# A fused attention block on one Trainium2 core: eight low-part operations given to GpSimd, one small result put in another PSUM bank, and every table of slots rewritten

## The reference, cut to what matters

```python
xn = layernorm(x)                                  # per row
q  = (layernorm(xn) * norm_g + norm_b) @ Wq        # 16 heads of 64
k, v = split(xn @ Wkv)
k, v = concat(null_k, k), concat(null_v, v)        # 2 more columns
q, k = l2norm(q) * q_scale, l2norm(k) * k_scale
sim  = 8 * q @ k.T - slope[h] * distance           # causal
x + softmax(sim) @ v @ Wout + layernorm(...)*ln_g + ln_b
```

## Time and profile before

| | us |
|---|---|
| median of 3 runs | 2699.43 (2696.95 to 2702.16) |
| the profiled execution | 2701.09 |
| its span | 2699.3 |

### The profile page before, as it was taken

One profiled execution on the slowest core, in us unless ns is written; L12 is line 12 of the kernel. 1 busy time (PEld: TensorE's weight loads), 2 busy tenths in 40 slices (PEclk: granted clock), 3 DMA queues, 4 the chain that ended last, 5 costly groups with the idle time before them and its releaser, 6 DMA issues.

```text
span 2699.3 us, 84329 instructions
## 1 busy us (share of the span) xinstructions
PE 2627.6 (97%) x31631; PEld 1578.7 (58%) x31631; DVE 2483.1 (92%) x6756; ACT 2127.0 (79%) x3385; POOL 2103.5 (78%) x2442
## 2 busy tenths in 40 slices
PE   5899999999999999999999999999999999999997
PEld 4456556565565565565565565566555665565654
DVE  8999998999989999999999999999999999989996
ACT  5688887888877888877888878788887888877876
POOL 6677887779867788678877788778887778877774
PEclk7899999999999999999999999999999999999999
DMA  5333354334544344433443436443453434544222
GB/s 170 74 67 72 79 105 98 89 73 82 100 100 94 69 87 97 98 85 78 96 103 82 89 75 102 102 92 72 78 106 89 101 71 78 100 102 74 57 56 71
DMA packets 638789, 236.94 MB, mean 88 GB/s; under 512 B 594608, under 2 KB 596656, under 8 KB 638384
## 3 DMA queue, kind: packets, MB, share of 16 engines
q1 hardware_dynamic: 636912, 231.45, 40.4%
q10 hardware_dynamic: 1472, 0.09, 0.0%
HBM read 72.01 MB, written 16.78 MB: 33 GB/s over the span
## 4 chain that ended last, share of the span: by engine, by line
PE 84%; DVE 7%; DMA 3%; issue 3%; POOL 2%; SPq 1%; ACT 1%; ACTq 0%; POOLq 0%; DVEq 0%
PE PS L1268 13%; PE PS L1245 12%; PE PS L1246 11%; PE PS L1247 11%; PE PS L1292 6%; PE PS L1331 6%; PE PS L1335 4%; PE PS L1333 4%; PE PS L1272 4%; PE PS L1358 4%; PE PS L1359 4%; PE PS L1360 4%; DVE PS L1044 2%; PE PS L1303 1%; DVE QKB L1064 1%
## 5 line engine op out<-in xcount | busy, mean ns | idle before, releaser
L1044 DVE CUSTOM_DVE_ANT_0 PS<-PS,STR 128x512 f32<-128x512 f32 (+3 forms) x1536 | 822.5, 580 | 124.3 <-PE PS L1292 117.4
L598 ACT ACTIVATE AR<-PS,SC 128x1024 f32<-128x1024 f32 (+1 forms) x640 | 655.0, 1023 | 146.5 <-PE PS L1303 76.8
L1245 PE MATMUL PS<-WH,XT 128*128 128x388 f16 x2048 | 677.3, 331 | 20.7 <-DVE AR L1057 10.8
L1246 PE MATMUL PS<-WL,XT 128*128 128x388 f16 x2048 | 674.6, 329 | 0.0
L1247 PE MATMUL PS<-WH,XT 128*128 128x388 f16 x2048 | 674.2, 329 | 0.0
L602 ACT ACTIVATE AR<-AR 128x1024 f16<-128x1024 f32 (+1 forms) x640 | 621.7, 971 | 20.3
L810 POOL TENSOR_TENSOR RN<-SS,HALF 128x8 f32<-128x8 f32 x256 | 453.6, 1772 | 179.2 <-DVE SS L1132 178.0
L1085 DVE TENSOR_TENSOR AR<-AR 128x768 f16<-128x768 f32 (+1 forms) x448 | 503.1, 1134 | 13.2 <-ACT AR L602 13.2
L1268 PE MATMUL PS<-AR 64*128 64x512 f16 (+3 forms) x4608 | 496.7, 324 | 9.2 <-ACT AR L598 9.2
L1331 PE MATMUL PS<-AR 128*128 128x66 f16 x4608 | 473.0, 195 | 2.1 <-DVE AR L1085 1.2
L1333 PE MATMUL PS<-AR 128*128 128x64 f16 x4608 | 469.4, 192 | 0.0
(11 more groups left out here) (227 smaller groups left out, 5199.7 us busy)
## 6 DMA issues: line engine op xcount, KB each, us to landing
XW<-in_L_attn_x SPq DMA_DIRECT2D x112, 256.0 KB, 3.1
XB<-in_L_attn_x SPq DMA_DIRECT2D x64, 256.0 KB, 2.9
out<-ACC SPq DMA_DIRECT2D x64, 256.0 KB, 2.3
ACC<-in_L_attn_x SPq DMA_DIRECT2D x56, 256.0 KB, 3.0
AR<-QKB SPq DMA_TRANSPOSE x512, 2.5
AR<-in_L_attn_Wkv SPq DMA_DIRECT2D x2, 1536.0 KB, 12.7
ACC<-in_L_attn_x SPq DMA_DIRECT2D x2, 1024.0 KB, 7.1
AR<-in_L_attn_Wout SPq DMA_DIRECT2D x1, 2048.0 KB, 8.3
```

The source lines that it names most:

```text
L598: e.activation(PR[:, n % 2, :, 0:wide], SB[:, :, 0:wide], ACT.Exp, scale=SIG).then_inc(s_p, 1)
L1044: e.tensor_tensor_reduce(out=r[:, 0:n], in0=r[:, 0:n], in1=ST[:, u % 2, h, o:o + n], scale=1.0, scalar=LOW, op0=ALU.add, op1=ALU.max, accu ...
L1245: e.matmul(to, XT[:, k, xs], WH[:, k, p, :], start=k == 0, stop=False)
L1246: e.matmul(to, XT[:, k, xs], WL[:, k, p, :], start=False, stop=False)
```

## The change

Three things. First, the low parts 8 to 15 of the late weights (the q weights of pairs 2 to 7) go from VectorE, one operation each, to GpSimd, two operations each: a multiplication in place and a subtraction. Their counts go to a semaphore of their own, `s_spq`, on which unit 1's turns into `KQ` and unit 2's first projection now wait. Second, the small transpose and product of the weights' maxima go to bank 5, and the transpose no longer waits until ScalarE has emptied the bias columns from bank 2. Third, all tables are new, `HOLD` too; the numbers of entries stay, apart from `W_LATD` and `W_LATP`.

```diff
@@ -48,68 +48,69 @@
 STEPS = [(qc, [(kt, 0)]) if kt < 4 * qc + 2 else (qc, [(kt, 0), (kt + 1, 256)]) for qc in range(2) for kt in range(4 * qc + 3)]
 NS = len(STEPS)
 PL_POOL = (0, 4, 7)
-W_PIECE = [47, 53, 56, 59, 66, 68, 69, 77, 79, 82, 83, 86]
-W_MAX = [41, 45, 49, 55, 64, 64, 66, 72, 75, 75, 76, 84]
-W_SCORE = [88, 96, 105, 108, 111, 115, 118, 126, 130, 133]
-W_PLOW = [94, 100, 101, 105, 108, 115, 122, 125, 131, 135]
-W_VALUE = [108, 109, 110, 116, 124, 127, 130, 136, 141, 149]
-W_NVP = [105, 115]
...
-W_OP = [121, 121, 138, 149, 160, 160, 167, 170]
-W_ADD = [117, 118, 136, 142, 158, 159, 167, 167]
-W_PROJ = [z for z in [7, 10, 17, 22, 26, 31, 37, 43] for k in range(KC)]
-W_KV = [5, 10, 16, 22, 28, 33, 39, 41]
-W_VL = [3, 7, 16, 21, 24, 27, 40, 42]
...
-W_SS = [13, 23, 36, 47]
-W_POW = [15, 28, 44, 47]
-W_TP = [25, 28, 59, 66]
-W_HI = [30, 37, 54, 68]
-W_LO = [26, 34, 52, 67]
...
-W_STAT = [-288, -194, -181, -174, -128, -113, -101, -96]
-W_XB = [-84, -74, -48, -28, -5, 8, 15, 17]
-W_XF = [-73, -53, -29, -6, -6, 11, 18, 20]
-W_XH = [-64, -25, -25, -4, 14, 14, 25, 28]
-W_XL = [-65, -33, -18, -4, 0, 10, 24, 25]
...
-HOLD = [2.0, 2.1, 2.0, 6.7]
...
-W_LATA = [-364, -352, -337, -320, -233, -223, -210, -207, -204, -202, -194, -152, -136, -103, -66, -55]
-W_LATD = [-313, -246, -231, -193, -187, -179, -171, -128, -96, -89, -73, -68, -67, 17, 19, 20]
-W_XF0 = [-177, -170]
-W_XH0 = [-73, 2]
-W_XL0 = [-78, -1]
-W_XT0 = [-106, -11]
-W_WOS = [-194]
-W_VNA = [-271, -123]
-W_VND = [-28]
-W_ALP = [-280, 32]
-W_ALA = [-116]
-W_WOM = [30, 40, 41]
-W_WOT = [46, 53]
-W_WOA = [51, 56, 56, 57]
-W_WOD = [54, 60, 60, 67]
+W_PIECE = [46, 52, 54, 62, 65, 68, 69, 79, 81, 84, 87, 90]
+W_MAX = [39, 44, 48, 53, 57, 63, 64, 71, 78, 82, 83, 84]
+W_SCORE = [92, 101, 104, 110, 112, 116, 122, 128, 132, 137]
+W_PLOW = [93, 98, 99, 104, 115, 115, 122, 126, 134, 136]
+W_VALUE = [109, 110, 111, 116, 129, 132, 132, 142, 149, 149]
+W_NVP = [106, 115]
...
+W_OP = [123, 123, 139, 146, 159, 161, 167, 171]
+W_ADD = [115, 117, 132, 140, 152, 156, 165, 166]
+W_PROJ = [z for z in [5, 12, 18, 22, 28, 35, 43, 46] for k in range(KC)]
+W_KV = [8, 13, 18, 21, 30, 35, 42, 46]
+W_VL = [4, 4, 15, 19, 28, 34, 40, 41]
...
+W_SS = [8, 22, 36, 45]
+W_POW = [21, 25, 43, 49]
+W_TP = [21, 42, 54, 67]
+W_HI = [29, 35, 56, 66]
+W_LO = [26, 38, 49, 64]
...
+W_STAT = [-296, -197, -192, -182, -161, -112, -105, -102]
+W_XB = [-111, -83, -61, -39, -15, -15, 14, 14]
+W_XF = [-82, -51, -32, -22, -6, -6, 8, 16]
+W_XH = [-78, -40, -25, -16, 3, 10, 17, 30]
+W_XL = [-60, -44, -14, -13, -4, 8, 13, 26]
...
+HOLD = [4.3, 4.4, 5.9, 7.6]
...
+W_LATA = [-378, -341, -321, -298, -184, -181, -179, -170, -170, -152, -122, -109, -93, -82, -60, -44]
+W_LATD = [-304, -283, -262, -179, -177, -155, -136, -135]
+W_LATP = [-99, -86, -76, -74, -30, 46, 73, 87]
+W_XF0 = [-161, -161]
+W_XH0 = [-43, 6]
+W_XL0 = [-56, -11]
+W_XT0 = [-68, -31]
+W_WOS = [-220]
+W_VNA = [-292, -166]
+W_VND = [-20]
+W_ALP = [-283, 28]
+W_ALA = [-166]
+W_WOM = [6, 8, 17]
+W_WOT = [36, 37]
+W_WOA = [30, 59, 66, 74]
+W_WOD = [40, 54, 68, 85]
 SLOTS = range(-500, SL * NU + 200)
 
 
@@ -305,7 +306,7 @@
         s_am, s_amt, s_dg, s_amb, s_wact, s_spl, s_tri = (mk("s_" + z) for z in ("am", "amt", "dg", "amb", "wact", "spl", "tri"))
         s_al, s_vsa, s_vn, s_scd, s_won, s_woh = (
             mk("s_" + z) for z in ("al", "vsa", "vn", "scd", "won", "woh"))
-        s_ready, s_ds, s_grp, s_one = mk("s_ready"), mk("s_ds"), mk("s_grp"), mk("s_one")
+        s_ready, s_ds, s_spr, s_spq, s_grp, s_one = mk("s_ready"), mk("s_ds"), mk("s_spr"), mk("s_spq"), mk("s_grp"), mk("s_one")
 
         s_x = [mk("s_x0"), mk("s_x1")]
         s_ax = [mk(f"s_ax{t}") for t in range(NT)]
@@ -463,7 +464,7 @@
                     if u > 1:
                         w.wait_ge(s_st, 2 * (NS * (u - 2) + (5, 7, 10, 10)[g]))
                     elif u:
-                        w.wait_ge(s_spl, 24)
+                        w.wait_ge(s_spq, 4)
                     w.wait_ge(s_lo, i + 1)
                     for t in range(2):
                         c = 256 * g + P * t
@@ -885,6 +886,12 @@
                         e.tensor_tensor(ALR, ALR, ALF, ALU.add).then_inc(s_al, 1)
                 for b, part in due_ln(s, W_SMALL):
                     ln_small(b, part)
+                for _, i in due(s, W_LATP, 1, BL):
+                    src, scale, hi, lo = late(8 + i)
+                    w.wait_ge(s_wact, 12 + 8 + i + 1)
+                    e.tensor_scalar(src, src, scale, None, ALU.mult).then_inc(s_spr, 1)
+                    w.wait_ge(s_spr, i + 1)
+                    e.tensor_tensor(lo, src, hi, ALU.subtract).then_inc(s_spq, 1)
 
         @block.vector
         def _(e):
@@ -983,12 +990,12 @@
             e.tensor_reduce(AM[:, 4:5], WV1, AXXY, ALU.max, apply_absolute_value=True).then_inc(s_am, 1)
             dc(e.tensor_scalar(W2R[:, :], QS[:, 0, :], SC[:, 1:2], QA / KA, ALU.mult, ALU.mult))
             w.wait_ge(s_amt, 1)
-            dc(e.tensor_reduce(M8, PS[0:8, 2, 192:320], AXX, ALU.max))
+            dc(e.tensor_reduce(M8, PS[0:8, 5, 0:128], AXX, ALU.max))
             e.tensor_scalar(DG, IDF[0:8, 0:8], M8, None, ALU.mult).then_inc(s_dg, 1)
             ln_xf(0, 2)
             ln_xf(0, 3)
             w.wait_ge(s_amb, 1)
-            top = PS[:, 2, 320:328]
+            top = PS[:, 5, 128:136]
             dc(e.tensor_scalar(AM[:, 8:9], top[:, 0:1], 1e-30, 1.0 / WS, ALU.max, ALU.mult))
             dc(e.tensor_reduce(AM[:, 9:10], top[:, 1:5], AXX, ALU.max))
             dc(e.tensor_scalar(AM[:, 9:10], AM[:, 9:10], 1e-30, 1.0 / WS, ALU.max, ALU.mult))
@@ -1223,10 +1230,9 @@
                                stop=k == KC - 1)
             ins.then_inc(s_bqn, 1)
             w.wait_ge(s_am, 1)
-            w.wait_ge(s_bqe, 3)
-            e.transpose(PS[0:8, 2, 192:320], AM[:, 0:8], IDF[:, :]).then_inc(s_amt, 1)
+            e.transpose(PS[0:8, 5, 0:128], AM[:, 0:8], IDF[:, :]).then_inc(s_amt, 1)
             w.wait_ge(s_dg, 1)
-            e.matmul(PS[:, 2, 320:328], ONE, DG, start=True, stop=True).then_inc(s_amb, 1)
+            e.matmul(PS[:, 5, 128:136], ONE, DG, start=True, stop=True).then_inc(s_amb, 1)
             w.wait_ge(s_ready, 1)
 
             def proj(u, j):
@@ -1239,7 +1245,8 @@
                     if u == 1:
                         w.wait_ge(s_spl, 12)
                     if u == 2:
-                        w.wait_ge(s_spl, 28)
+                        w.wait_ge(s_spl, 20)
+                        w.wait_ge(s_spq, 8)
                     bank_free(w, "pj", u, t)
                 to = rb("pj", u, t)[:, 0:WC]
                 e.matmul(to, XT[:, k, xs], WH[:, k, p, :], start=k == 0, stop=False)
```

## The result

The changed kernel takes 2718.41 us (median of 4 runs, 2716.01 to 2725.3), the kernel before 2699.27 in the same session (2696.95 to 2702.16): a ratio of 1.008, with a 95% interval of 1.0068 to 1.0092. It is slower by 19 us. 2697.0 was predicted, between 2680 and 2712, so the prediction failed, and its range with it.

What follows compares the result with a forecast made beforehand. In the middle TensorE's own stream of work sets the time. The terms 11.5 - 9.6 - 5 + 0.7 + 0 = -2.4 us on 2701.09 gave 2698.7, or 2697.0 against the median, range 2680 to 2712.

Steps and rivals of the forecast that it cites:

- Part 2: Middle units: piece 5's regular 0.16 us wait for piece 4's bank goes, -9.6 us over 60 units.
- Part 3: Batches' changes: pieces wait less for VectorE's maxima, -5 of 17 us extra, bounds -17 and +10.
- the prediction's own signs: Wrong if quiet units differ from 40.3 by over 0.1 us or unit 4's first projection moves over 5 us.
- Part 1: Middle units: two more passages between 64-row and 128-row work on TensorE, 0.096 us each, +11.5 us.
- Rival B: Middle: TensorE waits for maxima at other pieces, passages not paid for, +12.2 us or 2711.6; chance 0.16.
- Part 4: Start: bank -0.3, early maximum's chain +4.5, given back until unit 4 -3.5; together +0.7 us, from -5 to +9.
- the early maximum: Start: output weights' maximum in slot 6, not 30, ahead of unit 0's sums on VectorE; unit 1's projection +4.5 us.
- the cast's pace: Start: GpSimd's multiplications sized by its cast, 1024 in 1.04 us; its low parts 10 us in all, up to 19.
- Part 5: End: the last unit's chain stays nearly in the same slots, 0 us, ±3.
- Rival C: Start: the early maximum's wait on VectorE isn't made up, +8 in place of +0.7, 2704 to 2705; chance 0.10.
- Rival D: Start: GpSimd's new operations hold up VectorE's two-input ones for their whole length, +2 us or 2699; chance 0.42 shared with forecast.

Runs made afterwards that it cites:

- kernel 3: Kernel before with the last two k steps of projection tile 6 put behind piece 11, giving 22 passages a unit: 2707.32 us, ratio 1.004.
- kernel 7: Kernel before with only the maxima's transpose and product moved to bank 5, without their wait for bank 2: 2695.71 us, ratio 0.9993.
- kernel 8: Kernel before with bank 5 and low parts 8 to 15 on GpSimd, all other tables as before: 2702.24 us, ratio 1.0021.
- kernel 10: kernel 8 with seven of GpSimd's eight low parts moved behind unit 0's norms: 2699.04 us, ratio 1.0009.
- kernel 13: kernel 1 with group 2's K/Q high part at slot 54 (56) on ScalarE and low part at 47 (49) on VectorE: 2719.89 us, ratio 1.0081.
- kernel 1: Kernel before with all the new middle tables (W_PIECE to W_BA and HOLD) alone; start tables, low parts and bank as before: 2715.88 us, ratio 1.0069.

## Why the prediction was wrong

The step that failed is the one by which parts 2 and 3 turn waits into time: waits that go were counted as gained, -14.6 us, and the waits that come in their place were put at nothing. The runs showed that 14.3 us of waits went and 22.4 came, 13.8 of them at piece 4. Of the prediction's own signs, one spoke: unit 4's first projection is 5.7 us later, with 5 as the mark. The quiet units, at 40.2, are within its 0.1 of 40.3; what was lost lies in the other units.

*Part 1, passages, +11.5: right.* +11.3 us in the records, and kernel 3's quiet units show the price with nothing else moved. In its whole time 9.2 of the 11.3 are left.

*Part 2, the regular wait gone, -9.6: the wait went, its worth didn't.* Piece 5's waits fell by 6.2 us, piece 1's by 8.1. But I took the gain as the sum of waits that go, and named nothing that is late next. (The 3.1 us of work between the two pieces hold in the odd units alone, since an output tile stands there in every second unit; the 3.2 us that piece 5 still waits are all in even ones.) With pieces 4 and 5 moved apart, piece 4 itself comes sooner: over units 8 to 59 it begins 23.4 us behind tile 5's last matmul, 25.5 before, while the low part of its K/Q ends at 17.7 in both and SyncE's second transpose at 21.2 (21.5 before). The mean slack from the end of that issue to the piece fell from 4.0 to 2.2 us, and from the landing to the piece from 2.2 to 0.7. The means still fit; the units in which a turn lands 1 to 2 us late don't. I could have had this from the profile of before: a new slot of an instruction has to be held against every chain that ends there, K/Q's turn among them, and not against the wait alone that it has now.

*Part 3, the batches' changes, -5: wrong sign.* The mechanism came, and something else ate it. Waits for maxima did become rare (6.7 to 1.1 us), and the first units of the seven batches together take 4.2 us over 40.3 each, where they took 10.9. But the last units of the batches ahead of them take 13.5 in place of 3.2 and the last but one 5.6 in place of 1.7: 23.3 us in all in place of 15.8. The slow units of after: 44.4 us from 976.5 with 2.0 at K/Q's turn, 43.9 from 2081.7 with 2.0 at CT's, both with a fallen clock behind the wait.

The sum of parts 2 and 3 was -14.6; measured were +8.1 in waits, 2.2 less in the small gaps below 0.03 us. Rival B had the size (2711.6) and the shape, waits at other pieces that eat part 2; its mechanism, maxima in a new order, was not it. It had 0.16.

*Part 4, the start, +0.7: +5.7, with one step left out.* The bank gave what was said or somewhat more (the transpose waits for nothing; unit 4 at 194.0 in kernel 7, one profile). The chain of the early maximum came as it was told: VectorE stands 3.56 us, the first sums come 8 us later, and the first piece starts at 88.47, where 88 was forecast. What wasn't in it is the projection tile that the new tables put between the first two pieces, 3.7 us of the 4.1 by which unit 1's projection missed its 88.5. Of the 8.7 us, 3.0 came back until unit 4; 3.5 had been given back. GpSimd's share was mis-sized as well, but behind the maximum it hardly shows: I had its total at 10 us by the cast's pace, with 19 as its bound; it is 17.3 with every multiplication at its plain 1.56 us for 512, where the cast's pace gave 0.5 (the subtraction takes 1.16 to 1.21, 1.1 was taken), and 20 with the one that took 4.21. That made it end at 79.3, with the sums, and not some 5 us ahead of them. On the tables of before, without the early maximum, the same share costs 6.9 us (kernel 8). How much of the start the two would cost one without the other with the new tables is open.

*Part 5, the end, 0: +1.4,* within its bounds.

Rival C named the start at +8 for the maximum, at 0.10; the size was near, and the maximum's chain is a part of it. Rival D held that the two engines hold each other up. One L892 of 4.21 us is such a meeting: it starts at 64.42, while VectorE is in an L1151 (64.01 to 65.02) with L1155 straight behind it (64.94 to 67.28), both of two inputs, and ends 1.35 us behind them, at 68.63. That agrees with what the Trainium skill says of it (page SBUF — State Buffer, section SBUF: two separate sides): whichever of the two starts first keeps the other out for the whole instruction. But kernel 10 shows that about half of the share's cost or more is order.

## What to carry to other kernels

An order by hand that has been tuned as one is a set of slacks that belong together: a value matmul three slots earlier cost 138 us, a third of the tables (with the banks that they deal) taken alone 342. So a change of all of them can be predicted only by following, for each instruction that moves nearer to its producer, the slack of that chain and how widely it varies from unit to unit; that a present wait disappears is no gain until what comes late next is named. The slack to hold a new slot against is the one of the late cases: K/Q's turn lands after 2.5 us as a rule and after 4 in some units. And count issues on the DMA queue as work: a queue that is silent in the busy shares can be the one without room.

## What the runs showed of the hardware

**Issuing a transpose holds SyncE's queue** for 1.2 to 1.3 us, rarely more, as in the fence of kernel 13; the landing comes later (2.5 us from issue on the page). The Trainium skill names this as one way of being bound by DMA, an issuing engine whose own row is solid with DMA slices, "descriptor generation, not data movement" (page Perfetto Trace Analysis, section What "DMA-bound" means). In kernel 13 the queue is solid so from 1012.8 to 1022.5 us. That stretch can't tell the two by itself, since the 16 DMA engines, busy 41% of the whole span, have a share of 0.94 in it; but in the same run a transpose with no other directly ahead of it takes as long (median 1.23 us of 443, against 1.26 of the 517 that follow one).

**A turn's landing varies, and not with the load of the DMA engines alone.** From issue to landing the 474 turns of K/Q in the middle of the changed kernel take 2.3 us at least, 2.5 in the median and 5.0 at most; before it is 2.3, 2.5 and 4.7. The one issued at 984.1 landed after 4.1 us, with the DMA engines at a share of 0.05 from 986.0 to 988.3. No run tells why.

**The clock can fall after a stand of 2 us.** In the changed kernel piece 4 waited 1.97 us, and soon after a projection matmul took 0.32 us to the next in place of 0.165:

```profile
988.34 0.39 PE L1299 MATMUL PS<-AR 64*128 64x512 f16 x2 [1.97 <-DMA AR<-QKB]
...
989.33 0.33 PE L1253 MATMUL PS<-WL,XT 128*128 128x388 f16 x1
...
989.96 0.53 PE L1253 MATMUL PS<-WL,XT 128*128 128x388 f16 x1
990.29 0.53 PE L1254 MATMUL PS<-WH,XT 128*128 128x388 f16 x1
```

By stretches of that time (length; PE, PEld, DVE, ACT and POOL busy; granted clock) it is the lower of the two levels, 1.2 GHz, for some 3 us:

```profile
988.00:990.00 2.00, 1.66 (x10) 0.90 (x11) 1.97 (x4) 1.97 (x3) 1.69 (x2) 0.92 0.83 187
990.00:992.00 2.00, 2.00 (x10) 0.78 (x10) 1.06 (x4) 0.51 (x2) 1.94 (x4) 0.50 0.92 206
992.00:994.00 2.00, 2.00 (x28) 0.95 (x25) 0.34 (x3) 1.29 (x4) 2.00 (x2) 0.73 0.68 131
```

The same came behind the stand of 2.0 us that ended at 2118.1, with the clock low from 2119.5 to 2122.9. The two are some 3 of the 37.5 us of waits. But a third stand, the longest, cost nothing more (its end, and the stretch behind it):

```profile
1969.74 0.39 PE L1299 MATMUL PS<-AR 64*128 64x512 f16 x2 [2.18 <-DMA AR<-QKB]
...
1970.00:1972.00 2.00, 2.00 (x14) 1.09 (x12) 1.97 (x5) 1.49 (x2) 2.00 (x2) 1.00 0.86 224
```

TensorE had been busy for 2.2 of the 4 us until 988 and for 2.1 of those until 2118, and for 1.8 of those until 1970, where the clock stayed at 2.4 GHz. So a wait near 2 us can be paid nearly twice, and these rows don't tell when. That the slow level is the resting one and work releases it, as the Trainium skill has it (page TensorE: Matmul & The Clock Gate, section Part 1: The HAM clock gate), agrees with the return after 3 us of work.

**GpSimd pays for the order too.** Its short operation on the norms' weights took longer with the new middle tables in kernel 1, with nothing added to it; line L827 (count, then busy us and mean ns) before and in kernel 1:

```profile
L827 POOL TENSOR_TENSOR SQ<-SQ,W2R 128x256 f32<-128x256 f32 x256 | 188.7, 737 | 20.1
```

```profile
L827 POOL TENSOR_TENSOR SQ<-SQ,W2R 128x256 f32<-128x256 f32 x256 | 241.2, 942 | 20.1
```

That is 52 of the 102 us by which GpSimd is busier there. Its records tell why: 161 of the 256 take 0.73 us, as 253 do before, and 95 take 1.0 to 1.6. In 80 of the 95 VectorE was at the same time in the low part of an exponential (L1085, two inputs), in 15 of the 161, and in 2 of the 256 before. So it is a meeting of the two engines, as in the earlier trace rows, and the new order brings this pair together.
